# Second cross-attention: key roots as ACT's square root and DVE's reciprocal, in place of twelve DVE steps

## The chip, the cores and the metric

One core of a Trainium2 chip runs the whole program in one launch. Its engines are TensorE (PE in the profile, with PEld for its weight loads), VectorE (DVE), ScalarE (ACT), GpSimd (POOL) and SyncE (SP), which issues the transfers. Times are device microseconds of one execution; a kernel's time is the median of its runs.

## The reference, cut to what matters

The program is a two-layer perceiver block on x of 32 x 32 x 256 with a context of 32 x 257 x 256: cross-attention, self-attention, experts, and once more the same three kinds of stage. The change touches the second cross-attention, in which queries and keys are normalized head by head (16 heads of 16) before they are rotated:

```python
def rms_norm(x, w):
    var = jnp.mean(x * x, axis=-1, keepdims=True)
    return x * jax.lax.rsqrt(var + EPS) * w
...
q = rms_norm(q, q_norm_w)
k = rms_norm(k, k_norm_w)
q = apply_rope(q, q_cos, q_sin)
k = apply_rope(k, k_cos, k_sin)
attn = jax.nn.softmax(jnp.einsum('bhtd,bhsd->bhts', q, k) * scale, axis=-1)
out = jnp.einsum('bhts,bhsd->bhtd', attn, v)
return out.transpose(0, 2, 1, 3).reshape(B, T, C) @ Wo.T
```

EPS is 1e-06. For each of the 32 batches, 256 keys x 16 heads need one value 1/sqrt(sum of squares + 16e-06); the missing factor 4 of the mean is in the rotation's tables. (The 257th key of each batch is treated apart.)

## The kernel before, in words

All is f32. The second cross-attention (`cross(1)` on each engine) goes through the 32 batches one by one. A step s = 4n + j handles batch j of group n (8 groups of QB = 4); the groups 2 to 5 are run by a hardware loop, the others are written out. Every engine has its own instruction stream, written in the order of its `second_slot`, and the engines meet through semaphores named in `q`. In one step each engine works on several batches at once: `ahead(n, k, j, it, by)` gives the batch that lies `by` steps ahead.

What a step does to the keys, in the order of a batch's life: TensorE makes its raw keys 8 steps ahead (`keys`, L592, two banks of 256 columns) and ACT copies them out (L1090); 7 steps ahead ACT squares them (`squares`, L1104) and DVE sums each head (`sums`, L1491) into `kss`. `kss` holds a whole group: 128 x (4 batches x 2 halves x 16 heads) = 128 x 128. When the fourth batch of a group is summed, which happens in a step with j = 0, DVE takes the group's inverse roots at once (`inv_root`, L1526 to L1532): an addition, an integer estimate in two steps and three Newton rounds of three steps, each step waiting for the one before through the semaphore `root`. In the next step (j = 1) `norm` (L1515) scales the first batch of that group with them; it stands first in DVE's step. POOL rotates the scaled keys (`rope`, L1865 to L1869), TensorE turns them one step later (`turn_keys`, L603), and ACT copies them out (L1114), which empties the two banks that the step's `keys` then fill.

The attention of a step: TensorE's scores for the batch one ahead (L636), DVE's negated maxima in two halves (L1423), ACT's exponentials (L1139), TensorE's turning of the probabilities in two halves (`turns`, L650), copied by ACT (L1149) and by DVE (`turned`, L1442), the values (L614, copied by ACT at L1125), and the weighing (`weigh`, L667 and L671), which ends TensorE's step. ACT's step ends with `shared` (L1157), a copy of what L671 wrote. In j = 1 DVE also joins the group before (`join`, L1460 and L1465), in j = 2 it adds that group's output to x (L1472) and takes statistics. `merge` (L1450) multiplies a step's weighed values by their shares and `shares` (L1433) takes the reciprocals for that.

The first keys are made ahead of the steps: slots -8 to -3 run on TensorE, ACT and DVE at the tail of the first experts (`early`), the first group's root among them (slot -4), in front of DVE's additions of the experts' outputs (L1834).

ACT holds one set of functions at a time; the compiler puts a table load in front of an activation that needs another. The exponential (L1139) and the square root of the layer norms (L1059) each have such a load in this program; copies and squares do not.

Of the kernel before, what the change touches and what calls it, by code (L numbers as in the profile page):

```python
# [13 lines left out]
P = 128  # L14
# [113 lines left out]
def perceiver_block(nc, io, out):  # L128
    ctx = ExitStack()
    with ctx:  # L130
        def sb(name, shape, dt=F32):
            return ctx.enter_context(nc.sbuf_tensor(name, shape, dt))
# [139 lines left out]
        root_t = sb("root_t", [P, NT * NH])  # L272
        root_y = sb("root_y", [P, NT * NH], I32)
        qss = root_t
        qr = sb("qr", [P, NT * NH])


# [10 lines left out]
        def ahead(n, k, j, it, by):  # L288

            c = (j + by) // QB  # L290
            k2 = (k + c) % 2
            pair = (n + c - k2) // 2 if isinstance(n, int) else it + (k + c - k2) // 2
            return n + c, k2, (j + by) % QB, pair

        def there(n):

            return not isinstance(n, int) or 0 <= n < NT

        def batch(n, j):

            return QB * n + j
# [178 lines left out]
        def after(eng, sem, value):  # L480

            if not isinstance(value, int) or value > 0:
                eng.wait_ge(sem, value)
# [569 lines left out]
        def _(act):  # L1053
# [13 lines left out]
            def cross(l, early=False):  # L1067
# [83 lines left out]
                def shared(n, k, j, it):  # L1151

                    if not there(n):
                        return
                    b = batch(n, j)
                    act.wait_ge(q["pvw"], b + 1)
                    A(parts_of, bank[5][:, P:2 * P], copy).then_inc(q["partc"], 1)  # L1157

                def second_slot(n, k, j, it):
                    turned_keys(n, k, j, it, 0)  # L1160
                    turned(n, k, j, it)
                    turned_keys(n, k, j, it, 1)
                    squares(n, k, j, it)
                    keys(n, k, j, it, 0)
                    keys(n, k, j, it, 1)
                    exps(n, k, j, it, 0)
                    exps(n, k, j, it, 1)
                    values(n, k, j, it, 0)
                    values(n, k, j, it, 1)
                    shared(n, k, j, it)  # L1170

                def slot(n, k, j, it):
                    if l == 1:
# [190 lines left out]
        def _(dve):  # L1364
# [34 lines left out]
            def cross(l, early=False):  # L1399
# [68 lines left out]
                def added(n):  # L1468

                    dve.wait_ge(q["ow"], n + 1)  # L1470
                    xv = x.rearrange("p t d -> p (t d)")[:, bass.ds(n * D, D)]
                    ins = V.tensor_tensor(xv, xv, bank[5][:, 0:D], ALU.add)  # L1472
                    if isinstance(n, int) and n == NT - 1:
                        ins.then_inc(x_ready, 1)
                        return
                    ins.then_inc(q["xa"], 1)
                    dve.wait_ge(q["xa"], n + 1)
                    V.bn_stats(ln_stats.rearrange("p t s -> p (t s)")[:, bass.ds(n * 6, 6)],
                               x.rearrange("p t d -> p (t d)")[:, bass.ds(n * D, D)])

                def sums(n, k, j, it):

                    n2, k2, j2, pair = ahead(n, k, j, it, SUMS_AHEAD)
                    if not there(n2):
                        return
                    b2 = batch(n2, j2)
                    dve.wait_ge(q["sq"], b2 + 1)
                    if j2 == 0:

                        after(dve, q["root"], ROOT_STEPS * n2)  # L1490
                    V.tensor_reduce(kss[:, KW2 * j2:KW2 * j2 + KW2, :].rearrange("p w h -> p (w h)"),  # L1491
                                    ksq[j2 % 2].rearrange("p w (h d) -> p (w h) d", d=HD), AX_X, ALU.add).then_inc(q["ss"], 1)
                    if j2 < QB - 1:
                        return
                    dve.wait_ge(q["ss"], b2 + 1)

                    after(dve, q["kn"], QB * n2)
                    step = iter(range(1, ROOT_STEPS + 1))

                    def rooted(ins):  # L1500
                        ins.then_inc(q["root"], 1)
                        dve.wait_ge(q["root"], ROOT_STEPS * n2 + next(step))

                    flat = lambda v: v.rearrange("p t h -> p (t h)")
                    inv_root(flat(kr), flat(kss), QB * KW2 * NH, rooted)

                def norm(n, k, j, it):

                    n2, k2, j2, pair = ahead(n, k, j, it, NORM_AHEAD)
                    if not there(n2):  # L1510
                        return
                    b2 = batch(n2, j2)
                    after(dve, q["krope"], b2 - 1)
                    dve.wait_ge(q["kc"], KW2 * b2 + KW2)
                    V.tensor_tensor(kn[j2 % 2].rearrange("p w (h d) -> p (w h) d", d=HD),  # L1515
                                    kraw[k2][j2].rearrange("p w (h d) -> p (w h) d", d=HD),
                                    kr[:, KW2 * j2:KW2 * j2 + KW2, :].rearrange("p w h -> p (w h)").unsqueeze(2)
                                    .to_broadcast([P, KW2 * NH, HD]), ALU.mult).then_inc(q["kn"], 1)

                def inv_root(dst, src, w, step, r=P):  # L1520


                    v, t = root_v[0:r, 0:w], root_t[0:r, 0:w]
                    yi = root_y[0:r, 0:w]
                    y = yi.bitcast(F32)
                    step(V.tensor_scalar(v, src, 1e-6 * HD, None, ALU.add))  # L1526
                    step(V.tensor_scalar(yi, v.bitcast(I32), 1, None, ALU.logical_shift_right))
                    step(V.tensor_scalar(yi, yi, -1.0, float(0x5f3759df - 2 ** 31), ALU.mult, ALU.add))
                    for i in range(3):
                        step(V.scalar_tensor_tensor(t, v, 0.5, y, ALU.mult, ALU.mult))  # L1530
                        step(V.tensor_tensor(t, t, y, ALU.mult))
                        step(V.scalar_tensor_tensor(dst if i == 2 else y, t, 1.5, y, ALU.subtract, ALU.mult))  # L1532

                def second_slot(n, k, j, it):
                    n0, k0, j0, _ = ahead(n, k, j, it, -1)
                    norm(n, k, j, it)
                    if j == 1 and there(n) and not (isinstance(n, int) and n == 0):
                        join(n - 1)
                    if there(n0):
                        merge(n0, k0, j0)  # L1540
                    maxima(n, k, j, it, 0)
                    shares(n, k, j, it)
                    maxima(n, k, j, it, 1)
                    if j == OUT_SLOT and there(n) and not (isinstance(n, int) and n == 0):
                        added(n - 1)
                    turned(n, k, j, it)
                    sums(n, k, j, it)

                def slot(n, k, j, it):
                    if l == 1:  # L1550
# [499 lines left out]
```

## Time and profile before

| what | value |
|---|---|
| median of 3 runs | 1150.31 us (1144.82 to 1152.75) |
| profiled execution | 1141.98 us, of which the span of its instructions is 1140.1 us |
| busy in the span | PE 919.8 us (81%), PEld 744.6, DVE 504.1 (44%), ACT 465.6 (41%), POOL 322.3 (28%) |
| chain that ended last | PE 70%, DVE 15%, POOL 5% |
| mean granted TensorE clock | 0.895 of full speed |

A busy time is the sum over the whole program. The chain is the work followed back from the last instruction to what released it, step by step, so its shares say on which engine time was spent that nothing else could cover. The granted clock is the share of full speed (2.4 GHz) that TensorE had.

### The profile page before, as it was taken

What the parts mean: (1) busy time and instruction counts of PE and PEld (TensorE: products, weight loads), DVE (VectorE), ACT (ScalarE), POOL (GpSimd) and SP (SyncE); (2) the same over time, 40 slices, a digit from 0 to 9 for tenths busy, and PEclk for the clock granted to TensorE, in tenths of its full rate; (3) what the DMA queues carried; (4) which work ended last, traced back from release to release, by engine and by line L of the source; (5) the groups of instructions that cost most, each with busy time, mean ns of one, the idle gap of its engine ahead of it and who ended that gap; (6) DMA issues with size and microseconds to landing.
All of it is one profiled execution on the core that took longest, in us unless ns stands there. A gap on an engine that the chain in (4) does not pass through costs nothing.

```text
span 1140.1 us, 23919 instructions
## 1 busy us (share of the span) xinstructions
PE 919.8 (81%) x8634; PEld 744.6 (65%) x8634; DVE 504.1 (44%) x1454; ACT 465.6 (41%) x1370; POOL 322.3 (28%) x374
## 2 busy tenths in 40 slices
PE   5899999979785399999945399999986860799980
PEld 3677777644564199999934277777755650699970
DVE  3556656530564211111165567777765552122222
ACT  2677677623232033333233176777765630111100
POOL 2211121001100500000072467787861414000004
PEclk9999999979897599999977599999998865899995
DMA  8111126000000688888341011111000004699943
GB/s 253 62 40 39 38 72 216 3 1 0 1 1 1 237 309 326 323 323 329 132 153 37 1 39 39 39 39 37 0 2 2 2 1 168 221 336 336 336 164 106
DMA packets 50561, 135.75 MB, mean 119 GB/s; under 512 B 16168, under 2 KB 37552, under 8 KB 44464
## 3 DMA queue, kind: packets, MB, share of 16 engines
q1 hardware_dynamic: 47408, 126.28, 31.0%
q0 software_dynamic: 3072, 8.39, 2.2%
q8 instruction: 51, 0.84, 0.3%
q14 instruction: 30, 0.25, 0.1%
HBM read 117.35 MB, written 17.30 MB: 118 GB/s over the span
## 4 chain that ended last, share of the span: by engine, by line
PE 70%; DVE 15%; POOL 5%; issue 4%; ACT 2%; SPq 2%; DMA 2%; DVEq 0%; POOLq 0%; ACTq 0%
PE lower L1010 15%; PE upper L1019 10%; PE upper L592 9%; PE upper L614 8%; PE upper L650 5%; PE lower L636 3%; PE upper L667 3%; POOL xslot L1992 3%; PE upper L792 2%; DVE x L1834 1%; PE upper L687 1%; PE upper L603 1%; PE lower L535 1%; POOL arena L1998 1%; PE upper L671 1%
## 5 line engine op out<-in xcount | busy, mean ns | idle before, releaser
L1010 PEld LDWEIGHTS lower<-arena 128*128 128x128 f32 x1472 | 174.7, 195 | 6.1 <-DVE arena L1800 3.9
L1010 PE MATMUL lower<-arena 128*128 128x128 f32 x1472 | 175.5, 278 | 2.7 <-DVE arena L1800 2.7
L1019 PE MATMUL upper<-arena 128*128 128x256 f32 x552 | 126.4, 379 | 0.0
L1998 POOL DMA_INDIRECT arena<-yslot,slot x32 | 30.6, 957 | 322.9 <-DMA yslot<-arena 313.7
L614 PE MATMUL upper<-wkv,arena 128*128 128x256 f32 x512 | 121.4, 380 | 0.0
L1019 PEld LDWEIGHTS upper<-arena 128*128 128x128 f32 x552 | 101.5, 190 | 12.0
L614 PEld LDWEIGHTS upper<-wkv,arena 128*128 128x128 f32 x512 | 94.8, 191 | 11.6
L1341 ACT ACTIVATE arena<-lower,arena 128x128 f32<-128x128 f32 x184 | 52.5, 369 | 106.0 <-PE lower L1010 105.9
L650 PE MATMUL upper<-const,arena 128*128 128x128 f32 x512 | 80.2, 280 | 6.8 <-ACT arena L1149 6.2
L650 PEld LDWEIGHTS upper<-const,arena 128*128 128x128 f32 x512 | 59.7, 143 | 28.2 <-issue 12.4
L592 PE MATMUL upper<-wkv,arena 128*128 128x256 f32 x256 | 71.1, 412 | 4.8 <-DMA arena<-in_ctxT_dram 4.5
L1901 POOL TENSOR_TENSOR arena<-arena 128x512 f32<-128x512 f32 x64 | 67.4, 1066 | 14.6 <-DMA arena<-in_ctxT_dram 14.3
L1800 DVE COPY arena<-lower 128x256 f32<-128x256 f32 x46 | 19.3, 419 | 116.7 <-PE lower L994 116.7
L1139 ACT ACTIVATE arena<-arena 128x257 f32<-128x257 f32 x128 | 63.2, 498 | 2.2 <-DVE arena L1421 2.2
L1139 ACT ACTIVATE arena<-lower,arena 128x257 f32<-128x257 f32 x128 | 59.0, 480 | 10.0 <-DVE arena L1423 10.0
L592 PE MATMUL upper<-arena,wkv 128*128 128x257 f32 x256 | 62.2, 387 | 0.6 <-ACT vlast L1076 0.6
L1813 DVE COPY arena<-upper 128x256 f32<-128x256 f32 x46 | 19.5, 424 | 96.4 <-PE upper L1019 96.4
L1442 DVE COPY arena<-upper 128x512 f32<-128x512 f32 x64 | 43.9, 686 | 32.5 <-PE upper L650 32.5
L1347 ACT ACTIVATE arena<-lower 128x512 f32<-128x512 f32 x23 | 13.7, 597 | 106.6 <-PE lower L1010 106.6
L592 PEld LDWEIGHTS upper<-wkv,arena 128*128 128x128 f32 x256 | 48.4, 204 | 13.3 <-issue 5.4
L1992 POOL DMA_INDIRECT xslot<-xn,slot x32 | 31.1, 972 | 90.1 <-DVE tile_expert L1789 51.6
L636 PE MATMUL lower<-arena 32*64 32x257 f32 x1024 | 45.4, 411 | 13.4 <-POOL arena L1907 7.7
(230 smaller groups left out, 1624.6 us busy)
## 6 DMA issues: line engine op xcount, KB each, us to landing
arena<-in_ew_dram SPq DMA_DIRECT2D x23, 2048.0 KB, 7.2
arena<-in_ew_dram SPq DMA_DIRECT2D x23, 1536.0 KB, 6.2
arena<-in_ctxT_dram SPq DMA_DIRECT2D x16, 1028.0 KB, 5.2
xslot<-zero SPq DMA_DIRECT2D x2, 2944.0 KB, 15.2
arena<-xslot SPq DMA_DIRECT2D x46, 128.0 KB, 5.8
yslot<-arena SPq DMA_DIRECT2D x46, 128.0 KB, 6.1
const<-in_const_dram SPq DMA_DIRECT2D x1, 1152.0 KB, 7.7
x<-in_x_dram SPq DMA_DIRECT2D x1, 1024.0 KB, 5.6
```

The lines of the kernel that those rows point to most:

```text
L592: ins = mm(o, a, v, start=(c == 0), stop=(c == KC - 1))
L614: ins = mm(bank[6 + w][:, 0:D], dctx[k2][:, c, j2, w * P:w * P + P], wkv[l][:, c, D:2 * D], start=(c == 0), stop=(c == KC - 1))
L636: ins = mm(bank[i][64 * c:64 * c + 64, 0:S], xq[k2][rows, c, j2, :, :].rearrange("p e q -> p (e q)"), ktb[j2 % 2][rows, c, :], start=True, ...
L650: ins = nc.tensor.transpose(bank[4][:, i * P:i * P + P], prob[j % 2][:, i, w * P:w * P + P], ident)
L1010: ins = mm(bank[1 + half][:, i * P:i * P + P], ew[k][:, at:at + P], exT[k % 2][:, c, :], start=(c == 0), stop=(c == KC - 1))
L1019: ins = mm(bank[4 + k % 2][:, 0:D], eh[k % 2][:, i, :], ew[k][:, at:at + D], start=(i == 0), stop=(i == nh - 1))
L1139: A(prob[j2 % 2][:, i, :], src, ACT.Exp, bias=negmax[j2 % 2][:, i:i + 1], accum_out=rowsum[j2 % 2][:, i:i + 1]).then_inc(q["probs"], 1)
L1341: ins = A(eh[k % 2][:, c, :], bank[1 + half][:, i * P:i * P + P], ACT.Gelu_apprx_tanh, bias=eb1[k][:, c:c + 1])
L1442: V.tensor_copy(probT[j % 2][:, 1, :, :].rearrange("p i q -> p (i q)"), bank[4][:, :]).then_inc(q["turnc"], 1)
L1901: G.tensor_tensor(dctx[k2][:, :, j2, :], of[:, :, 0:LASTKEY], of[:, :, LASTKEY:S].to_broadcast([P, KC, LASTKEY]), ALU.subtract).then_inc(q ...
L1992: G.indirect_dma_start(out=xslot[l], out_offset=at(i, t), in_=xn[:, t, :], in_offset=None)\
L1998: G.indirect_dma_start(out=eyg[t][i], out_offset=None, in_=yslot[l], in_offset=at(i, t))\
```

## The change

DVE keeps the first of the twelve steps, the addition of 16e-06, at the end of the step with j = 0, as soon as the group's sums are there. ACT takes the square root of the whole group into a new tile `key_sd` at the end of the same step, behind `shared`. DVE takes the reciprocal at the beginning of the next step, in front of `norm`. The semaphore `root` now counts additions, and `sqrt` and `inverse` are new. On DVE `sums` now stands ahead of `turned`. The roots of the queries and of the last keys keep their twelve steps.

```diff
@@ -272,6 +272,7 @@
         root_t = sb("root_t", [P, NT * NH])
         root_y = sb("root_y", [P, NT * NH], I32)
         qss = root_t
+        key_sd = sb("key_sd", [P, QB * KW2 * NH])
         qr = sb("qr", [P, NT * NH])
 
 
@@ -1156,6 +1157,15 @@
                     act.wait_ge(q["pvw"], b + 1)
                     A(parts_of, bank[5][:, P:2 * P], copy).then_inc(q["partc"], 1)
 
+                def roots(n, k, j, it):
+
+                    n2, k2, j2, pair = ahead(n, k, j, it, SUMS_AHEAD)
+                    if not there(n2) or j2 != QB - 1:
+                        return
+                    act.wait_ge(q["root"], n2 + 1)
+                    after(act, q["inverse"], n2)
+                    A(key_sd[:, :], root_v[:, 0:QB * KW2 * NH], ACT.Sqrt).then_inc(q["sqrt"], 1)
+
                 def second_slot(n, k, j, it):
                     turned_keys(n, k, j, it, 0)
                     turned(n, k, j, it)
@@ -1168,6 +1178,7 @@
                     values(n, k, j, it, 0)
                     values(n, k, j, it, 1)
                     shared(n, k, j, it)
+                    roots(n, k, j, it)
 
                 def slot(n, k, j, it):
                     if l == 1:
@@ -1487,22 +1498,15 @@
                     dve.wait_ge(q["sq"], b2 + 1)
                     if j2 == 0:
 
-                        after(dve, q["root"], ROOT_STEPS * n2)
+                        after(dve, q["root"], n2)
                     V.tensor_reduce(kss[:, KW2 * j2:KW2 * j2 + KW2, :].rearrange("p w h -> p (w h)"),
                                     ksq[j2 % 2].rearrange("p w (h d) -> p (w h) d", d=HD), AX_X, ALU.add).then_inc(q["ss"], 1)
                     if j2 < QB - 1:
                         return
                     dve.wait_ge(q["ss"], b2 + 1)
-
-                    after(dve, q["kn"], QB * n2)
-                    step = iter(range(1, ROOT_STEPS + 1))
-
-                    def rooted(ins):
-                        ins.then_inc(q["root"], 1)
-                        dve.wait_ge(q["root"], ROOT_STEPS * n2 + next(step))
-
-                    flat = lambda v: v.rearrange("p t h -> p (t h)")
-                    inv_root(flat(kr), flat(kss), QB * KW2 * NH, rooted)
+                    after(dve, q["sqrt"], n2)
+                    V.tensor_scalar(root_v[:, 0:QB * KW2 * NH], kss.rearrange("p t h -> p (t h)"), 1e-6 * HD, None, ALU.add)\
+                     .then_inc(q["root"], 1)
 
                 def norm(n, k, j, it):
 
@@ -1510,6 +1514,12 @@
                     if not there(n2):
                         return
                     b2 = batch(n2, j2)
+                    if j2 == 0:
+
+                        after(dve, q["kn"], b2)
+                        dve.wait_ge(q["sqrt"], n2 + 1)
+                        V.reciprocal(kr.rearrange("p t h -> p (t h)"), key_sd[:, :]).then_inc(q["inverse"], 1)
+                        dve.wait_ge(q["inverse"], n2 + 1)
                     after(dve, q["krope"], b2 - 1)
                     dve.wait_ge(q["kc"], KW2 * b2 + KW2)
                     V.tensor_tensor(kn[j2 % 2].rearrange("p w (h d) -> p (w h) d", d=HD),
@@ -1543,8 +1553,8 @@
                     maxima(n, k, j, it, 1)
                     if j == OUT_SLOT and there(n) and not (isinstance(n, int) and n == 0):
                         added(n - 1)
+                    sums(n, k, j, it)
                     turned(n, k, j, it)
-                    sums(n, k, j, it)
 
                 def slot(n, k, j, it):
                     if l == 1:
```

In the built program ACT's stream around one group's roots, from the copy at the end of a step with j = 0 to the first of the next step's exponentials, in the loop. Here and below L-numbers of the changed kernel are some lines higher: L1157 of before is L1158, L1114 is L1115, L1149 is L1150, L1104 is L1105, L1090 is L1091, L1139 is L1140. Before:

```order
L1157 ACTIVATE arena<-upper 128x128 [waits cross1_pvw]
L1114 ACTIVATE arena<-upper 128x2x128 [waits cross1_scores,cross1_tw]
L1149 ACTIVATE arena<-upper 128x512 [waits cross1_pvw,cross1_turnw]
L1114 ACTIVATE arena<-upper 128x2x128 [waits cross1_scores,cross1_tw]
L1104 ACTIVATE arena<-arena 128x512 [waits cross1_ss,cross1_kc]
L1090 ACTIVATE arena<-upper 128x256 [waits cross1_kn,cross1_kw] x2
L1139 ACTIVATE arena<-lower,arena 128x257 [waits cross1_recip,cross1_turnw,cross1_negmax]
```

The same stretch of ACT in the changed kernel:

```order
L1158 ACTIVATE arena<-upper 128x128 [waits cross1_pvw]
L1167 ACT_TABLE_LOAD [waits cross1_inverse]
L1167 ACTIVATE key_sd<-root_v 128x128 [waits cross1_root]
L1115 ACTIVATE arena<-upper 128x2x128 [waits cross1_scores,cross1_tw]
L1150 ACTIVATE arena<-upper 128x512 [waits cross1_pvw,cross1_turnw]
L1115 ACTIVATE arena<-upper 128x2x128 [waits cross1_scores,cross1_tw]
L1105 ACTIVATE arena<-arena 128x512 [waits cross1_ss,cross1_kc]
L1091 ACTIVATE arena<-upper 128x256 [waits cross1_kn,cross1_kw] x2
L1140 ACT_TABLE_LOAD [waits cross1_recip,cross1_turnw]
L1140 ACTIVATE arena<-lower,arena 128x257 [waits cross1_negmax]
```

Two table loads and the square root have come in; the waits for `recip` and `turnw` stand on the second load now, and only the wait for the maxima (`negmax`) is left on the exponential.

DVE's stream at the same place, from the end of a step with j = 0 to the scaling that begins the next. Before, with nine of the twelve root steps left out:

```order
L1442 COPY arena<-upper 128x512 [waits cross1_pvw,cross1_turnw]
L1487 ISA
L1491 TENSOR_REDUCE arena<-arena 128x32 [waits cross1_sq]
L1526 TENSOR_SCALAR root_v<-arena 128x128 [waits cross1_kn,cross1_ss]
L1502 ISA
L1527 TENSOR_SCALAR root_y<-root_v 128x128 [waits cross1_root]
...
L1532 SCALAR_TENSOR_TENSOR arena<-root_t,root_y 128x128 [waits cross1_root]
L1502 REGISTER_ALU
L483 REGISTER_ALU [waits cross1_root]
L1514 ISA [waits cross1_krope]
L1515 TENSOR_TENSOR arena<-arena 128x512 [waits cross1_kc]
```

In the changed kernel (L1502 was L1491, L1508 was L1526, L1453 was L1442, L1525 was L1515; ISA and REGISTER_ALU rows prepare waits):

```order
L1502 TENSOR_REDUCE arena<-arena 128x32 [waits cross1_sq]
L1508 TENSOR_SCALAR root_v<-arena 128x128 [waits cross1_sqrt,cross1_ss]
L1451 ISA
L1453 COPY arena<-upper 128x512 [waits cross1_pvw,cross1_turnw]
L1520 REGISTER_ALU [waits cross1_kn]
L1521 RECIPROCAL arena<-key_sd 128x128 [waits cross1_sqrt]
L484 REGISTER_ALU [waits cross1_inverse]
L1524 ISA [waits cross1_krope]
L1525 TENSOR_TENSOR arena<-arena 128x512 [waits cross1_kc]
```

Before, L1442 stood ahead of L1491, and between L1491 and L1515 stood the twelve steps; now there is one addition, and in front of the scaling a reciprocal that waits for ACT.

## Rows read from the trace of the kernel before

A row of the table of windows has the window, its length, busy time and count for PE, PEld, DVE, ACT and POOL, the granted clock, the DMA share and GB/s; the windows below are s1, s5, s6, s9, s13 and s14. A row of the timeline has the start, the length, engine, line and operation, and in brackets the idle time before it with what ended it. A row of the groups has the count, the busy time, the mean ns of one and the idle time before.

**Rows 1.** Table of windows, each from one start of L667 to the next.

```profile
664.83:671.25 6.42, 6.42 (x85) 5.00 (x84) 6.15 (x16) 4.97 (x19) 3.02 (x4) 1.00 0.01 3
690.58:699.21 8.63, 6.49 (x85) 5.03 (x85) 8.11 (x21) 5.11 (x20) 4.46 (x5) 1.00 0.01 2
699.21:708.04 8.83, 8.83 (x89) 6.96 (x89) 5.67 (x11) 4.97 (x19) 6.23 (x9) 0.81 0.00 0
721.10:728.41 7.31, 6.50 (x85) 5.03 (x85) 6.68 (x18) 5.11 (x19) 3.48 (x4) 1.00 0.00 1
748.64:756.41 7.77, 6.50 (x85) 5.04 (x85) 7.10 (x20) 5.12 (x20) 3.48 (x4) 1.00 0.00 1
756.41:763.70 7.29, 7.29 (x89) 5.77 (x89) 5.20 (x11) 4.96 (x19) 7.21 (x9) 1.00 0.01 3
```

**Rows 2.** Timeline of s13 on DVE: start, length, engine, line, operation.

```profile
747.48 0.45 DVE L1526 TENSOR_SCALAR root_v<-arena 128x128 f32<-128x128 f32 x1
...
751.92 0.69 DVE L1515 TENSOR_TENSOR arena<-arena 128x512 f32<-128x512 f32 x1 [0.23 <-DVE arena L1532]
...
755.59 0.68 DVE L1442 COPY arena<-upper 128x512 f32<-128x512 f32 x1
...
756.18 0.67 DVE L1491 TENSOR_REDUCE arena<-arena 128x32 f32<-128x512 f32 x1
```

**Rows 3.** Timeline of s13 on ACT.

```profile
749.63 0.32 ACT L1157 ACTIVATE arena<-upper 128x128 f32<-128x128 f32 x1
...
750.54 0.39 ACT L1114 ACTIVATE arena<-upper 128x256 f32<-128x256 f32 x1 [0.59 <-PE upper L603]
...
753.45 0.38 ACT L1090 ACTIVATE arena<-upper 128x256 f32<-128x256 f32 x1 [0.59 <-PE upper L592]
...
755.04 0.48 ACT L1139 ACTIVATE arena<-lower,arena 128x257 f32<-128x257 f32 x1 [1.21 <-DVE arena L1423]
```

**Rows 4.** Timeline of s13 on TensorE: keys and weighing.

```profile
751.00 1.11 PE L592 MATMUL upper<-wkv,arena 128*128 128x256 f32 x4
...
756.41 0.65 PE L667 MATMUL upper<-arena 128*32 128x64 f32 x32 [1.27 <-DVE arena L1442]
```

**Rows 5.** Timeline of ACT at its first exponentials of this stage.

```profile
655.83 1.28 ACT L1139 ACT_TABLE_LOAD   x1
657.12 0.48 ACT L1139 ACTIVATE arena<-lower,arena 128x257 f32<-128x257 f32 x1
```

**Rows 6.** Groups of instructions on DVE: its reciprocals of 4 and 16 columns.

```profile
L1433 DVE RECIPROCAL arena<-arena 128x4 f32<-128x4 f32 x64 | 11.0, 172 | 0.0
...
L1631 DVE RECIPROCAL srcp<-ssum 128x16 f32<-128x16 f32 x8 | 2.0, 253 | 0.3
```

**Rows 7.** Timeline of s1, s5, s9 and s25: ACT and DVE.

```profile
665.82 0.32 ACT L1157 ACTIVATE arena<-upper 128x128 f32<-128x128 f32 x1
...
669.91 0.47 ACT L1139 ACTIVATE arena<-lower,arena 128x257 f32<-128x257 f32 x1
...
691.57 0.32 ACT L1157 ACTIVATE arena<-upper 128x128 f32<-128x128 f32 x1
...
694.25 0.69 DVE L1515 TENSOR_TENSOR arena<-arena 128x512 f32<-128x512 f32 x1
...
722.09 0.32 ACT L1157 ACTIVATE arena<-upper 128x128 f32<-128x128 f32 x1
...
723.93 0.69 DVE L1515 TENSOR_TENSOR arena<-arena 128x512 f32<-128x512 f32 x1 [0.23 <-DVE arena L1532]
...
832.84 0.28 ACT L1157 ACTIVATE arena<-upper 128x128 f32<-128x128 f32 x1
...
835.32 0.69 DVE L1515 TENSOR_TENSOR arena<-arena 128x512 f32<-128x512 f32 x1
```

**Rows 8.** Timeline at the first root: ACT and DVE.

```profile
586.80 0.39 ACT L1090 ACTIVATE arena<-upper 128x256 f32<-128x256 f32 x1 [0.41 <-PE upper L592]
...
590.59 0.69 DVE L1515 TENSOR_TENSOR arena<-arena 128x512 f32<-128x512 f32 x1
```

## The prediction

> **What bounds the kernel now.** I read the page first. TensorE leads it, but its busy share is a mean over six stages, and the change touches one: the second cross-attention, which runs from about 650 to 875 us in 32 steps, here s0 to s31 (s = 4n + j). The next view is the table of windows, cut from one start of the weighing matmuls (L667) to the next [rows 1]. A step that waits for nothing takes 6.42 us and TensorE is busy through all of it. From s5 on one in four (j = 1: s5, s9, s13, s17, s21, s25) takes longer, 8.63 us in s5, 7.31 in s9 and 7.77 in s13, with the same 6.5 us of matmul: TensorE stands idle for the rest, 2.14, 0.81 and 1.27 us. The timeline of s13 tells why. DVE begins the twelve-step root at 747.48 [rows 2], and the scaling of the next keys (L1515) cannot start before 751.92. Behind it on DVE stand join, merge, the maxima and the copy of the turned probabilities (L1442), and that copy is what the weighing matmuls wait for: 756.41, after 1.27 us idle [rows 4]. ACT waits too, 1.21 us, for the maxima [rows 3]. So in these steps the path runs over DVE, and the root is on it. s1 has a root before it as well but no join, and took 6.42 us: there nothing was lost.
>
> **What is removed.** Eleven DVE instructions of each of eight roots; an addition remains. In s13 this frees DVE for some 4 us. At most these steps could return to 6.42: 2.2 us in s5, 0.9 in s9, 1.35 in s13 and in its likes s17 and s21, 7 us in all, and something in s25, which has no keys to make.
>
> **What is added, on ACT.** The root is not asked for where DVE's addition ends but at the end of ACT's step, behind L1157, which ends at 749.95 in s13 [rows 3]; I call this moment E. The built order shows a table load in front of the square root and another in front of the next exponential. A table load took 1.28 us, and the exponential began right behind it, 1.29 after the load's start [rows 5]. The square root of 128x128 I take at 0.31 us, from ACT's copy of that size, 0.32 [rows 3]. So the roots are ready at E + 1.6. ACT's next instruction, the copy of turned keys, began at E + 0.59 because it waited for TensorE; now it begins at E + 1.6, 1.0 late. The key matmuls that wait for the bank which this copy empties go from 751.00 [rows 4] to 752.0, and ACT's last copy before the exponentials, which ended at 753.83 [rows 3], ends at 754.85. There the second load begins: the waits that stand on it (the reciprocal and the turns of the step before) were met long ago, and only the exponential itself waits for the maxima. It ends at 756.13, where the first exponential began at 755.04: **+1.1 us by ACT**. Two loads and a root are 2.87 us, of which the two idle times of ACT, 0.59 and 1.21, hide 1.8.
>
> **What is added, on DVE.** The addition runs early, behind the sums in the step before; it is hidden, since DVE now has 3 us to spare until E + 1.6. The reciprocal stands first in the next step and everything on DVE is queued behind its wait for the root. Its price has no row: DVE's reciprocals took 172 ns for 4 columns and 253 for 16 [rows 6], 6.75 ns a column, which for 128 columns gives 0.253 + 112 x 0.00675 = 1.0 us. The low bound is a plain operation of this shape, 0.45 [rows 2]; the high one 1.2, if each of the 128 columns cost 8 ns on top of the 0.17 of the smallest. I take 1.0, since the two rows are of the operation itself. With 0.04 to hand over and the 0.23 that DVE waits for its own result ahead of L1515 [rows 2], scaling starts at 749.95 + 1.6 + 0.04 + 1.0 + 0.23 = 752.82, 0.9 later than now. So the four microseconds that DVE saves are spent waiting for ACT.
>
> **What is moved.** The sums (L1491) now stand ahead of the copy L1442. In steps j = 0 and 3 TensorE is still at its values when the copy runs, and the shift is covered; at j = 2 the copy waits for the addition of the output and the cover is nearly used up, and I count 0. At j = 1 the copy is what TensorE waits for, and the sums cost their whole spacing, 756.18 - 755.59 = 0.59 [rows 2]. No DMA is moved, and POOL, which starts each rotation on the scaled keys, is busy for 3.48 of the 7.77 us of s13 [rows 1].
>
> **The sum.** In s13 the copy comes 0.9 + 0.6 = 1.5 us later; that is more than ACT's 1.1, so DVE decides: +1.5, and as much in s17 and s21, where E and L1515 stand the same way within 0.1: 4.5. s9 [rows 7]: E = 722.41, scaling at 725.28 in place of 723.93, +1.35 + 0.6 = 1.95. s5: E = 691.89; its row of L1515 shows no wait, so with 0.04 in place of 0.23 it is 694.57 in place of 694.25, +0.3 + 0.6 = 0.9. s25: E = 833.12, in the same way 835.8 in place of 835.32, and no sums are left: +0.5. s1: its exponentials began at 669.91 without waiting for DVE; by the ACT chain they begin at E + 6.18 = 666.14 + 6.18 = 672.32: +2.4. The first root lies ahead of the steps, in the tail of the experts: ACT is free at 587.19 [rows 8], so root 588.78, reciprocal to 589.82, scaling at 589.87 in place of 590.59: -0.7, and DVE's additions of the experts' outputs stand right behind it. Together 4.5 + 1.95 + 0.9 + 0.5 + 2.4 - 0.7 = **+9.6 us**. With the reciprocal at 0.45 ACT's bound decides in s13 and its likes (3 x 1.1), s9 1.5 (exponentials at E + 6.18 = 728.59 where L1515 and 3.12 as in s13 give 727.05), s5 0.4, s25 0, s1 2.4, the first -1.25: +6.3. At 1.2 it is 0.2 more in all but s1, +11.0.
>
> The profiled execution took 1141.98 us (span 1140.1 and 1.9 around it); the median of the three runs is 1150.31, 0.7% above it. The sum makes the execution 1151.6 and the median 1160.
>
> **Weighed against the Trainium skill.** In the trace the load occupies ACT for 1.28 us, it began with no idle time in front, and the exponential follows at once [rows 5]. "ScalarE: Activation LUTs", section "What ACT_TABLE_LOAD costs", gives 1283 ns for the load and about 1380 ns more for a drain, 2.66 us a switch. The load agrees; the drain does not appear in these rows. By that page the sum would be the last rival's.
>
> **Rivals.** (a) *TensorE's clock falls in the gaps.* After s5, with its 2.14 us of idle time, the next step ran at a mean granted clock of 0.81 and took 8.83 us; s14, behind 1.27 us, ran at 1.00 in 7.29 [rows 1]. A fall costs 1.5 us. In s9, s13, s17 and s21 TensorE will be idle for 2.7 us or more, but in two pieces, 1.0 at the key matmuls and some 1.8 ahead of the weighing. Against it: 1.8 is nearer to what passed than to 2.14, and s5 may lose its fall by the same splitting. If all four fall: +15.6, 1166. (b) *Not slower: ACT has room after all.* Were a load 0.3 us or less, so that load and root fitted ACT's first gap of 0.59, and the reciprocal 0.45, scaling would start 0.65 earlier than now in s13, the swap would eat that, and s5, s25 and the first root would give some 4 us: 1146. Against it: every load in the trace took 1.28. (c) *A switch costs 1.38 us more than the load shows*, because ACT empties first. Then DVE's side grows by 1.38 and ACT's by 2.76: s13 and its likes 3.9 each and s9 4.3 by ACT, s5 2.3 and s25 1.9 by DVE, s1 5.2, the first +0.7: +26.1, 1176.
>
> **How the numbers follow.** Forecast +6 to +11 with 1160: 0.62. Clock (a): 0.20. (b): 0.04. (c): 0.05. The rest, 0.09, is a smaller loss, 0 to +5, if part of the delay is caught up in the steps behind. One per cent is 11.5 us, about what a measurement of this kernel can tell from no change. The runs shown lie up to 5 us off their median, so the forecast passes 11.5 in a third of its cases (0.20), (a) mostly (0.17), (c) always (0.05): slower 0.42. Faster needs (b) and a lucky run: 0.03. The range takes in the low end with the smaller losses and (a) with the spread of the runs: 1151 to 1170.
>
> **What would show it.** In the changed profile: a 1.28 us table load behind L1157's copy and another ahead of the exponentials at each j = 1; DVE idle for 3 to 4 us until ACT's square root ends; a reciprocal of about 1.0 us; j = 1 steps of about 9.3 us (s13) and s1 of 8.8; the weighing matmuls still waiting for DVE's copy. I am wrong if the exponentials' load waits for the maxima (then 1.3 us more in each step), if the reciprocal is under 0.6 or over 1.3 us, or if the steps behind are shorter than 6.42 and give the delay back.

## The result, and the profile after

The changed kernel took 1161.18 us (median of 4 runs, 1156.98 to 1161.76), the kernel before beside it 1147.57 (4 runs, 1142.43 to 1152.75): a ratio of 1.009 with a 95% interval of 1.0051 to 1.0129. Two later comparisons gave 1.0046 (1.003 to 1.0063) and 1.0075 (1.0045 to 1.0104). So it is slower, by some 0.5 to 0.9%, less than the 1% that the prediction calls about what a measurement can tell from no change. The profiled execution took 1161.76 us with a span of 1159.9; DVE's busy time fell from 504.1 to 483.0 us and ACT's rose from 465.6 to 485.8. What that costs TensorE stands in the rows below.

First the table of windows of the kernel after, each from one start of the weighing matmuls (L668 now) to the next, with the columns of [rows 1]: s1, s2, s5, s6, s9, s13, s14.

```profile
671.65:679.16 7.51, 6.68 (x85) 5.07 (x85) 4.44 (x9) 6.53 (x17) 2.65 (x3) 1.00 0.01 2
679.16:686.78 7.62, 6.50 (x84) 5.04 (x84) 4.09 (x8) 6.24 (x23) 7.53 (x9) 1.00 0.01 2
...
699.68:709.26 9.58, 6.68 (x85) 5.07 (x85) 6.37 (x12) 8.42 (x25) 4.71 (x6) 1.00 0.01 2
709.26:718.02 8.76, 8.76 (x89) 6.77 (x89) 5.25 (x10) 4.48 (x15) 5.63 (x7) 0.81 0.00 1
...
731.06:740.29 9.23, 6.68 (x86) 5.08 (x86) 5.90 (x12) 8.31 (x24) 4.08 (x4) 1.00 0.00 0
...
760.50:769.72 9.22, 6.68 (x85) 5.07 (x85) 5.89 (x12) 8.30 (x24) 4.08 (x4) 1.00 0.00 0
769.72:778.60 8.88, 8.88 (x89) 7.12 (x89) 4.58 (x10) 4.75 (x17) 6.74 (x9) 0.81 0.01 3
```

Against [rows 1] s13 has grown from 7.77 to 9.22 with the same matmuls in it, while DVE is busy for 1.2 us less and ACT for 3.2 us more. s1, which lost nothing before, has 7.51 in place of 6.42, and s2 another 1.19 too much. s14 also grew, from 7.29 to 8.88, for another reason: its granted clock is 0.81.

Where s13 goes is in the timeline of ACT, in the places of [rows 3]:

```profile
761.49 0.32 ACT L1158 ACTIVATE arena<-upper 128x128 f32<-128x128 f32 x1
761.83 1.28 ACT L1167 ACT_TABLE_LOAD   x1
763.12 0.31 ACT L1167 ACTIVATE key_sd<-root_v 128x128 f32<-128x128 f32 x1
763.34 0.37 ACT L1115 ACTIVATE arena<-upper 128x256 f32<-128x256 f32 x1
...
766.23 0.39 ACT L1091 ACTIVATE arena<-upper 128x256 f32<-128x256 f32 x1 [0.84 <-PE upper L593]
766.63 1.28 ACT L1140 ACT_TABLE_LOAD   x1
767.93 0.48 ACT L1140 ACTIVATE arena<-lower,arena 128x257 f32<-128x257 f32 x1
```

The load begins 0.02 behind E = 761.81, the root ends 1.62 behind it, and the second load stands right behind the last copy of keys and waits for nobody. In the timeline of DVE in the same step, in the places of [rows 2]:

```profile
758.77 0.83 DVE L1508 TENSOR_SCALAR root_v<-arena 128x128 f32<-128x128 f32 x1
...
763.46 0.95 DVE L1521 RECIPROCAL arena<-key_sd 128x128 f32<-128x128 f32 x1 [3.26 <-ACT key_sd L1167]
764.64 0.69 DVE L1525 TENSOR_TENSOR arena<-arena 128x512 f32<-128x512 f32 x1 [0.23 <-DVE arena L1521]
...
768.30 0.68 DVE L1502 TENSOR_REDUCE arena<-arena 128x32 f32<-128x512 f32 x1
768.90 0.68 DVE L1453 COPY arena<-upper 128x512 f32<-128x512 f32 x1
```

DVE is idle for 3.26 us until the root; that is most of the some 4 us that the eleven instructions took which are gone. Then reciprocal and hand-over put the scaling 2.83 us behind E, where [rows 2, 3] had it 1.97 behind, and the sums stand ahead of the copy for 0.60 more. TensorE in the same step, in the places of [rows 4]:

```profile
763.76 1.13 PE L593 MATMUL upper<-wkv,arena 128*128 128x256 f32 x4 [0.74 <-ACT arena L1115]
...
769.72 0.65 PE L668 MATMUL upper<-arena 128*32 128x64 f32 x32 [1.80 <-DVE arena L1453]
```

It waits twice: 0.74 us for the copy that the load holds up, and 1.80 for DVE's copy. In s1 and s2 it waits for ACT both times, first for the same copy and then for the exponentials behind the second load:

```profile
674.91 1.13 PE L593 MATMUL upper<-wkv,arena 128*128 128x256 f32 x4 [0.74 <-ACT arena L1115]
...
681.16 0.69 PE L637 MATMUL lower<-arena 32*64 32x257 f32 x16 [1.12 <-ACT arena L1140]
```

### The profile page after: what moved, and what is told of

Same layout as the page of the kernel before. It is cut to its first block, busy times and chain, and to the rows that moved or that the text cites. A ratio compares the mean times of both kernels' runs of the same rounds, so it can differ in the third digit from the quotient of the medians.

```text
span 1159.9 us, 23827 instructions
## 1 busy us (share of the span) xinstructions
PE 928.5 (80%) x8634; PEld 750.9 (65%) x8634; DVE 483.0 (42%) x1374; ACT 485.8 (42%) x1392; POOL 321.6 (28%) x374
## 4 chain that ended last, share of the span: by engine, by line
PE 69%; DVE 13%; issue 5%; ACT 4%; POOL 4%; SPq 2%; DMA 2%; another core or an unknown queue 1%; DVEq 0%; POOLq 0%; ACTq 0%
PE lower L1011 14%; PE upper L1020 10%; PE upper L593 9%; PE upper L615 7%; PE upper L651 5%; PE lower L637 3%; PE upper L668 3%; POOL xslot L2002 3%; PE upper L793 2%; DVE x L1844 1%; PE upper L688 1%; PE upper L604 1%; ACT arena L1140 1%; PE lower L536 1%; PE upper L970 1%
## 5 line engine op out<-in xcount | busy, mean ns | idle before, releaser
L615 PE MATMUL upper<-wkv,arena 128*128 128x256 f32 x512 | 121.5, 380 | 0.0
L615 PEld LDWEIGHTS upper<-wkv,arena 128*128 128x128 f32 x512 | 95.0, 191 | 11.9
L593 PE MATMUL upper<-wkv,arena 128*128 128x256 f32 x256 | 75.9, 431 | 15.2 <-ACT arena L1091 5.9
L593 PEld LDWEIGHTS upper<-wkv,arena 128*128 128x128 f32 x256 | 50.8, 215 | 26.9 <-ACT arena L1091 7.4
L1140 ACT ACTIVATE arena<-arena 128x257 f32<-128x257 f32 x128 | 63.2, 497 | 2.6 <-DVE arena L1432 2.6
L1140 ACT ACTIVATE arena<-lower,arena 128x257 f32<-128x257 f32 x128 | 59.0, 480 | 2.6 <-DVE arena L1434 2.5
L1917 POOL TENSOR_TENSOR arena<-qT,const 128x256 f32<-128x256 f32 x32 | 22.7, 711 | 120.9 <-PE lower L637 114.1
```

What stands on the lines that cost most here:

```text
L593: ins = mm(o, a, v, start=(c == 0), stop=(c == KC - 1))
L615: ins = mm(bank[6 + w][:, 0:D], dctx[k2][:, c, j2, w * P:w * P + P], wkv[l][:, c, D:2 * D], start=(c == 0), stop=(c == KC - 1))
L1140: A(prob[j2 % 2][:, i, :], src, ACT.Exp, bias=negmax[j2 % 2][:, i:i + 1], accum_out=rowsum[j2 % 2][:, i:i + 1]).then_inc(q["probs"], 1)
```

## The experiments

**DVE's copy ahead of the sums again** (the swap undone).

```diff
-                    sums(n, k, j, it)
                     turned(n, k, j, it)
+                    sums(n, k, j, it)
```

> The changed kernel with DVE's copy of the turned probabilities ahead of the sums again. Of my theory (the weighing matmuls of a j = 1 step wait for DVE's queue, and the sums cost their spacing of 0.60 there): s9, s13, s17 and s21 8.6 to 8.75 in place of 9.22, s5 9.0 to 9.1 in place of 9.58, s24 5.5 in place of 5.85, s1 unchanged at 7.5; 2.5 to 3.3 us in all, 1158.5 where the changed kernel has 1161. If ACT's exponentials behind the table load set these steps and not DVE's copy, none of them moves: 0.

Measured: 1150.34 us (10 runs) where the kernel before had 1151.25 and the changed one, on the same chip, 1157.11; ratio to the kernel before 0.9988 (0.9973 to 1.0003). The windows of s13 and s14:

```profile
758.26:766.88 8.62, 6.67 (x85) 5.07 (x85) 5.29 (x11) 7.70 (x21) 3.48 (x4) 1.00 0.00 0
766.88:774.17 7.29, 7.29 (x88) 5.77 (x88) 5.09 (x11) 5.12 (x19) 7.21 (x9) 1.00 0.01 3
```

s5, s9, s13, s17 and s21 each came down by 0.60 (8.98, 8.63, 8.62, 8.62, 8.63), s24 by 0.34; s1 and s2 together stayed at 15.13. So DVE's queue sets the j = 1 steps, and the sums cost there what stands in [rows 2]. The steps gave 3.3 us, the run 6.8. Another 3 are the clock, with no rule for it yet: the steps behind s5 and s13 (s6 and s14) ran at full clock here, 7.28 and 7.29 in place of 8.76 and 8.88. Against the kernel before the steps are still 7 us longer (s6, s14 and s26 aside, where the clock falls), and yet the time is 1 us shorter; the table on the runs' clock, below, takes this up. TensorE's idle time ahead of the weighing in s13 was 1.21 us here and 1.80 in the changed kernel.

**A copy in place of the square root**, and so no change of table.

```diff
-A(key_sd[:, :], root_v[:, 0:QB * KW2 * NH], ACT.Sqrt).then_inc(q["sqrt"], 1)
+A(key_sd[:, :], root_v[:, 0:QB * KW2 * NH], copy).then_inc(q["sqrt"], 1)
```

> The changed kernel with a copy on ACT in place of the square root: the keys' roots are left out, and with them both table loads of each group; the reciprocal, the place of the work and all waits stay. Of my theory (the loads make the root late and hold up the exponentials) the scaling of the keys starts 0.31 + 0.04 + 0.95 + 0.23 = 1.5 us behind E in place of 2.8: s13, s17 and s21 7.9 to 8.0 in place of 9.22, s9 7.9, s5 8.4, s25 7.7 in place of 8.88, s1 and s2 6.42 each in place of 7.5 and 7.6; 9 to 10 us less in the steps and 1.3 in the early root, about 1150 where the changed kernel has 1161 and the one before 1148. Of the rival (the reciprocal at the head of DVE's step and the order of DVE are the cost, the loads lie in ACT's idle time): at most 3 us less, with s13 at 9.2 less what the root's 1.28 alone gives back, 8.9 or more, and s1 unchanged. If each load also cost 1.38 for emptying ACT, which the records would not show, 20 us or more would come back.

Measured: 1145.55 us, 11.6 under the changed kernel on the same chip; ratio to the kernel before 0.9942 (0.9919 to 0.9964). The windows of s1 and s13, then ACT and DVE in s13:

```profile
671.68:678.11 6.43, 6.43 (x86) 5.01 (x85) 4.79 (x9) 5.18 (x20) 2.98 (x4) 1.00 0.01 3
...
753.92:761.72 7.80, 6.50 (x85) 5.03 (x85) 5.89 (x12) 5.91 (x23) 4.08 (x4) 1.00 0.00 0
```

```profile
754.91 0.32 ACT L1158 ACTIVATE arena<-upper 128x128 f32<-128x128 f32 x1
755.07 0.36 ACT L1167 ACTIVATE key_sd<-root_v 128x128 f32<-128x128 f32 x1
...
759.76 0.48 ACT L1140 ACTIVATE arena<-lower,arena 128x257 f32<-128x257 f32 x1 [0.65 <-DVE arena L1434]
```

```profile
755.46 0.95 DVE L1521 RECIPROCAL arena<-key_sd 128x128 f32<-128x128 f32 x1 [1.84 <-ACT key_sd L1167]
756.64 0.69 DVE L1525 TENSOR_TENSOR arena<-arena 128x512 f32<-128x512 f32 x1 [0.23 <-DVE arena L1521]
```

s1 and s2 went back to 6.43 and 6.42, s13, s17 and s21 to 7.80, and DVE and ACT wait for each other again as in [rows 3]. Each group from s5 on had lost 1.42 by the load ahead of the root: 1.28 of the load and 0.14 because the square root behind a load begins when the load is over, while the copy here began 0.16 before the one ahead of it ended. That is the whole price: with the 1.38 more of the last rival the steps would have given back about twice as much. The reciprocal and the swap, still there, cost what the saved steps give, and that leaves s13 where it was, at 7.80 here and 7.77 before. (This run leaves the square root out, so its keys are not the kernel's.)

**The swap alone, on the kernel before.** The root is taken out of the sums, so that only they move.

```diff
-                    turned(n, k, j, it)
                     sums(n, k, j, it)
+                    turned(n, k, j, it)
+                    rooting(n, k, j, it)
```

> The kernel before with one part of the change alone: the sums stand ahead of DVE's copy of the turned probabilities, the twelve-step root stays where it was behind both. Of my theory the sums' spacing of 0.60 is on the path in the j = 1 steps: s5 9.2 in place of 8.63, s9 7.9 in place of 7.31, s13, s17 and s21 8.35 in place of 7.75, s24 5.8 in place of 5.52; +3 to +3.3 us, 1151 where the kernel before has 1148. If the copy has room there, 0.

Measured: s5 9.13, s9 7.93, s13 8.18, s17 7.97, s21 8.18: 0.50, 0.62, 0.41, 0.27 and 0.38 more than before; s24 5.52, unchanged. The window of s13:

```profile
755.39:763.57 8.18, 6.50 (x86) 5.04 (x86) 7.54 (x20) 5.71 (x22) 4.08 (x4) 1.00 0.00 1
```

The direction is as expected and the size 2.2 us in place of 3: with the copy between the sums and the root's first addition, the addition of s13 begins 0.09 earlier in the step and took 0.34 where [rows 2] have 0.45 (why it is shorter is not shown), so the scaling comes 0.2 earlier and gives some of it back. The run as a whole took 1148.11 beside 1151.25, a ratio of 0.9974 (0.9955 to 0.9993): the 2.2 us do not show in the total, which is 5 us lower than they make it. The table on the runs' clock, below, shows where most of these 5 us are.

**The load one instruction earlier** (on the kernel with the copy ahead of the sums).

```diff
                     keys(n, k, j, it, 0)
+                    if j == 1 and there(n):
+                        nc.scalar.preload_act_table_set("exp_and_others")
                     keys(n, k, j, it, 1)
```

> The kernel with DVE's copy ahead of the sums (turned_first), and the table of the exponential loaded one instruction earlier, between the two copies of new keys, where ACT stands idle for 0.84 us anyway. Of my theory s1 and s2 are set by this load (together 15.13 us there, 12.85 before), so they come down by about the 0.84 that is hidden, to 14.3; s13, s17 and s21 are set by DVE's queue behind the root and stay at 8.62, s9 too; 0.8 us in all. If the exponentials behind the load set the j = 1 steps as well, these come down by up to 0.8 each, to 7.8, and 4 us are gained.

Measured: 1155.15 us, ratio 1.0053 (1.0017 to 1.009). The windows of s1, s2 and s13:

```profile
672.10:679.71 7.61, 6.87 (x85) 4.96 (x84) 4.55 (x9) 7.55 (x21) 2.75 (x4) 1.00 0.01 2
679.71:686.34 6.63, 6.53 (x86) 5.05 (x85) 4.41 (x8) 5.11 (x19) 6.55 (x8) 1.00 0.02 5
...
757.39:766.01 8.62, 6.94 (x85) 4.99 (x85) 5.29 (x11) 7.88 (x23) 3.48 (x4) 1.00 0.00 0
```

s1 and s2 take 14.24 together, 0.89 less, and s13 stays at 8.62. So the load ahead of the exponentials sets s1 and s2, where DVE has no join to do, and has room in the others. The added line loads the table in the last group too, which has no root: s30 took 6.45 us, 5.95 without it. The total can't tell 0.9 us; the profiled execution also had its clock down for longer in s26 (9.31 us, 7.73 in the kernel with the swap undone).

**Both kernels again**, for what is the change's and what is chance.

> The changed kernel once more, to see what of its profile repeats. Of the queue on DVE (my theory): s13, s17 and s21 at 9.2 us and s9 at 9.2, s5 at 9.6, s1 and s2 at 7.5 and 7.6, as in the first profile, since nothing there is left to chance. Two things in the first profile are not of that theory: ACT's two stalls of 2.48 and 4.53 us in the early keys (at 590 and 595 us) and the fall of the granted clock in s14 (8.88 us at 0.81). If the stalls belong to the new program they stand here again, at the same instructions; if they are chance, the experts' stage with the early keys is 6 to 8 us shorter than in the first profile. If the clock falls behind every 1.8 us of idle time by chance, another step than s14 may show it, or none.

> The kernel before once more. Its steps in the second cross-attention should repeat within 0.1 us (s5 8.63, s6 8.83, s13 7.77, 272.3 us from the layer norm ahead of this stage to the one behind it), and the ratio should hold 1. In the first profile the stage of the experts with the early keys took 255.2 us; in all other profiles so far, also in one in which ACT's program is that of the kernel before, it took 260.0 to 263.7, with idle times of ACT of 2.5 and 4.5 us in the early keys that no instruction ends. If these belong to the change, this profile has 255 again; if they come and go in every kernel, it may have 260 to 264, and then the 8.4 us by which the two first profiles differ there are not the change's.

> The same kernel a third time, only for its profile: steps as before within 0.1 us, and one more value of the stage with the early keys, 255 or 260 to 264.

> The changed kernel again, in more rounds, since its two ratios so far, 1.0090 and 1.0046, leave open how much of the loss of the steps reaches the whole. Of my theory the steps lose 10.4 us (with the granted clock falling as it may, in a kernel of either kind), and the early root gives 0.7 to 2.9 back: +7.5 to +9.7, a ratio of 1.0065 to 1.0085. A ratio of 1.004 or less would say that half of what the steps lose is made up elsewhere. The profile's steps should repeat within 0.1 us except where the clock falls.

Measured: the kernel before against itself 1.0008 (0.9976 to 1.0041). The steps repeat: in the three profiles of after every step from s1 to s25 agrees within 0.03 us, in those of before within 0.06, but for s6. That one ran at 0.81 in two profiles of before (8.83 and 8.79) and at full clock in the third (7.29). In the three profiles of after s6 and s14 always fell, s10, s18 and s22 never, though TensorE had been idle for 1.80 or 1.81 us ahead of all of s10, s14, s18 and s22. In s26 it was down in all six, for different lengths: 7.86, 10.53 and 7.74 before, 9.26, 9.26 and 7.68 after.

The stage of the experts with the early keys, from the square root of one layer norm (L1059) to that of the next, took 255.2, 267.2 and 264.2 us in the three profiles of before and 263.6, 260.0 and 260.2 in those of after. ACT's idle times that no instruction ends ("remote") are in both kernels; here in the second profile of the kernel before:

```profile
588.11 0.38 ACT L1090 ACTIVATE arena<-upper 128x256 f32<-128x256 f32 x1 [3.17 <-remote]
...
593.74 0.38 ACT L1090 ACTIVATE arena<-upper 128x256 f32<-128x256 f32 x1 [4.58 <-remote]
```

So the 8.4 us by which the first two profiles differ in that stage are not the change's: the first profile of before was the lucky one. One thing in this stage is the change's: the early root. DVE and POOL in the second profile of before:

```profile
598.38 0.23 DVE L1526 TENSOR_SCALAR root_v<-arena 128x128 f32<-128x128 f32 x1
598.63 0.94 DVE L1527 TENSOR_SCALAR root_y<-root_v 128x128 int32<-128x128 int32 x1
...
601.68 1.01 DVE L1531 TENSOR_TENSOR root_t<-root_t,root_y 128x128 f32<-128x128 f32 x1
602.73 0.29 DVE L1532 SCALAR_TENSOR_TENSOR root_y<-root_t,root_y 128x128 f32<-128x128 f32 x1
...
605.01 0.69 DVE L1515 TENSOR_TENSOR arena<-arena 128x512 f32<-128x512 f32 x1
```

```profile
597.38 5.16 POOL L1901 TENSOR_TENSOR arena<-arena 128x512 f32<-128x512 f32 x5
```

Four of the twelve steps took about 1 us in place of 0.23 to 0.29 while POOL's additions ran (five in 5.16 us, also some 1 us each), and the steps behind them 0.29 again. From addition to scaling it took 3.72, 6.63 and 6.76 us in the three profiles of before, and 3.77, 4.38 and 3.77 in those of after. The lengths of the stage are too few and too scattered to show this gain.

**What the runs' own clock says.** Every run has its mean granted clock, and the times go with it. The 62 runs of the kernel before have medians of 1154.4 us at 0.889, 1151.2 at 0.893, 1146.9 at 0.899 and 1143.0 at 0.903: 0.7 us less for each 0.001 more. A straight line through them leaves a scatter of 1.2 us where the times alone have 3.5. The first profile of before, 1141.98 us at 0.895, lies 8 us below the line. The last column of the table has how far each kernel's runs lie from the line at their own clock, with a 95% interval; one run of the load one instruction earlier, at 0.861, and two of 1927.83 and 2988.66 us are left out. Beside it stands what the profiles give: the steps without s6, s14 and s26, and the first root, from addition to scaling, against 6.1 us, the mean of the four profiles that have twelve steps there.

| kernel | steps | first root | together | runs at equal clock |
|---|---|---|---|---|
| changed | +10.4 | -2.2 | +8.2 | +9.0 (0.6 either way) |
| copy ahead of the sums | +7.0 | -2.4 | +4.7 | +4.7 (0.9) |
| a copy in place of the square root | -0.4 | -3.8 | -4.2 | -3.5 (1.2) |
| the swap alone | +2.1 | 0 | +2.1 | +2.0 (0.8) |
| the load one instruction earlier | +6.6 | -2.4 | +4.3 | +5.2 (0.9) |
| logarithm and exponential (below) | -7.7 | -4.4 | -12.1 | -12.0 (1.3) |

So steps and first root account for the runs within 1 us, and the change costs 9 us, or 0.8%, beside the clock. Each of the three comparisons gives this by itself (9.3, 8.7 and 9.0), though their ratios stand for 10.3, 5.3 and 8.6. What moves the clock of a run is not shown; the 1.6 us of s14's fall are in the main not in the 9.

**The root on ACT without a change of table** (on the kernel with the copy ahead of the sums): logarithm and exponential from one table, no reciprocal on DVE. The table is loaded ahead of the early keys and again behind the layer norm.

```diff
-                    after(act, q["inverse"], n2)
-                    A(key_sd[:, :], root_v[:, 0:QB * KW2 * NH], ACT.Sqrt).then_inc(q["sqrt"], 1)
+                    after(act, q["kn"], QB * n2)
+                    A(key_sd[:, :], root_v[:, 0:QB * KW2 * NH], ACT.Ln).then_inc(q["inverse"], 1)
+                    act.wait_ge(q["inverse"], n2 + 1)
+                    A(kr.rearrange("p t h -> p (t h)"), key_sd[:, :], ACT.Exp, scale=-0.5).then_inc(q["sqrt"], 1)
...
+                    nc.scalar.preload_act_table_set("natural_log_exp_and_others")
...
+                    nc.scalar.preload_act_table_set("natural_log_exp_and_others")
```

> The root wholly on ACT without a change of table: a logarithm and an exponential of minus half of it, both from one table that is loaded ahead of the stage and serves the softmax too; no reciprocal on DVE, and DVE's copy ahead of the sums. Of my theory (what costs is that the root comes late, by the load and the reciprocal, and that the exponentials wait for a load) the scaling starts at E + 0.8 in place of E + 2.8 after and E + 2.0 before: s13, s17 and s21 6.6 in place of 7.7 before, s9 6.6, s5 7.1, s1 6.5, s25 7.0, with no fall of the clock in s6 (7.3) and less in s26 (6.4): 10 us under the kernel before, 1140 where that has 1150. If what costs is only that ACT has another instruction at the end of its step, or if the rotation on POOL sets the j = 1 steps once DVE is out of the way, s13 stays at 7.3 or more and 4 us at most are gained.

Measured: 1133.55 us beside 1147.30, a ratio of 0.9877 (0.9829 to 0.9926): faster than both kernels. The windows of s5 and s13, then ACT and DVE in s13:

```profile
696.07:702.91 6.84, 6.50 (x85) 5.03 (x85) 4.82 (x10) 5.62 (x22) 4.11 (x4) 1.00 0.01 2
...
750.05:756.62 6.57, 6.49 (x85) 5.03 (x85) 4.36 (x10) 5.62 (x22) 3.49 (x4) 1.00 0.00 0
```

```profile
751.04 0.32 ACT L1158 ACTIVATE arena<-upper 128x128 f32<-128x128 f32 x1
751.20 0.36 ACT L1167 ACTIVATE key_sd<-root_v 128x128 f32<-128x128 f32 x1
751.59 0.31 ACT L1169 ACTIVATE arena<-key_sd 128x128 f32<-128x128 f32 x1
751.94 0.39 ACT L1115 ACTIVATE arena<-upper 128x256 f32<-128x256 f32 x1
```

```profile
752.12 0.69 DVE L1526 TENSOR_TENSOR arena<-arena 128x512 f32<-128x512 f32 x1 [2.79 <-ACT arena L1169]
```

Scaling starts 0.76 behind E. s9, s13, s17 and s21 take 6.56 or 6.57, all but the 6.42 of a step that waits for nothing; s5 takes 6.84, s25 6.75, s1 6.43. Against the first profile of before that is 7.7 us in the steps, and 3.0 in s6 and s26, which kept their clock: 10.7, and the interval of the ratio, 8 to 20 us, holds that; the 3.0 of the clock are not sure to be the kernel's, since s6 kept its clock in the third profile of before as well. The Trainium skill, "ScalarE: Activation LUTs", section "Table sets: the hidden batching unit", lists the exponential and the square root in different sets, and one set that has exponential and logarithm; the trace agrees on both, with two loads a group above and none within the stage here.

## Why the prediction was right

**The path.** DVE still decides the j = 1 steps, now through its wait for ACT's root: the 3.26 us of idle time stand where the prediction put 3 to 4, and undoing the swap moved these steps, by the 0.60 expected, and besides them only s24. In s1 it is ACT, as said, though the loss is split: s1 took 7.51 where the prediction has 8.8, and s2, which it does not name, 7.62. Moving the second load gave 0.89 back there and nothing in s13.

**The terms.** Forecast and measured against the first profile of before: s1 with s2 +2.4 and +2.28; s5 +0.9 and +0.95; s9 +1.95 and +1.92; s13, s17 and s21 +1.5 each and +1.45, +1.52 and +1.42; s25 +0.5 and +0.51. The reciprocal of 128 columns, which had no row, took 0.95 us; the line through the two rows of [rows 6] gave 1.0.

**What was missed.** s24 (j = 0) lost 0.33: there the cover that was counted on for the sums and the addition was not enough. The first root was put at -0.7; it was 0 against the first profile of before and -2.3 to -3.0 against the other two, in which POOL's additions slowed DVE's steps, a thing the first profile did not show. The steps without s6, s14 and s26 are +10.4 together; with some 2 us back by the first root +8 remain, and the runs at equal clock say +9.0. The forecast of +9.6 was near, and partly because these two errors have opposite signs. That the forecast time of 1160 lies so close to the 1161.18 measured is luck besides: it stands on a median of 1150.31 for the kernel before, which was 1147.57 beside the changed one, and the changed kernel's later medians are 1157.11 and 1157.68. How the stage of the experts varies by up to 12 us with the same program is not settled; it is why one profile says little here.

**The rivals.** (a) came true for one gap of the four: s14 fell and cost 1.6 us (8.88 for 7.29), in all three profiles, which the forecast sum does not hold; the fall behind s5 stayed. Not falling behind s9, s17 and s21 after the same 1.80 us was not foreseen and stays open. (b) would have needed a load of 0.3; it took 1.28. (c) is refuted by the copy in place of the square root: no time beyond the load and 0.14 us of lost overlap came back. The Trainium skill, "ScalarE: Activation LUTs", section "What ACT_TABLE_LOAD costs", has the load right (1283 ns, 1.28 us here); its 1380 ns for a drain appear in no row and in no difference between runs here.

## What to carry to other kernels

Moving work to an engine with idle time gained nothing here, because the result was due at a place where that engine is late: count from when the helper can start, not from how long it takes. A new table function among exponentials cost two loads here, one of which delayed the new result by 1.42 us and the other the next exponential, which TensorE felt in s1 and s2 alone; look for the same function from a table that serves both. Price a reordered instruction at the one step where nobody covers it, and read steps, not totals, when the total varies by more than the effect, or set totals beside each other at the same granted clock.

## What was not expected of the hardware

- An activation overlapped the one before it by about 0.16 us here, but not a table load: the square root began 1.29 behind the load's start, the copy in its place 0.16 before its predecessor's end.
- DVE's operations on 128 columns took 0.94 to 1.05 us in place of 0.23 to 0.29 beside POOL's additions of 128x512 (second and third profile of before), though not each: L1526 took 0.23 in the same stretch of the second. The Trainium skill, "GPSIMD Engine Reference", section "Specifications", says that GpSimd shares its SBUF interfaces with VectorE, with contention for DVE instructions that have two inputs there or run in a two-port mode; the slow steps with two inputs fit that; L1526 to L1528 have one, and no run here shows which mode they ran in.
- The granted clock of the next step fell to 0.81 behind 1.80 us of idle time in s13 in all three profiles of after, and behind the same idle time in s9, s17 and s21 in none. With at most 1.68 us there, in all other profiles, it fell in none. Whether the idle time is what makes it fall is not shown.
